# Attention and expert layers on one core: another order of the work between the last scores and the first expert tile

## The reference

```python
x = x + xattn(layernorm(x), ctx)      # 16 x 224 tokens of 512, context 16 x 750 of 384, 16 heads of 32
x = x + ffn(layernorm(x))
# ffn: logits = cos(x, centroids) + x @ w_route.T          (8 experts)
#      gates  = softmax over the top 2 of the logits
#      h      = gelu(x @ w1[e] + b1[e])                    (512 -> 256)
#      out    = sum over the two e of gates[e] * (h @ w2[e] + b2[e])
```

## Time and profile before

| | |
|---|---|
| median of 3 runs | 1463.79 us (1462.31 to 1467.72) |
| profiled execution, its own time | 1467.88 us |
| its span | 1466.0 us |
| mean granted clock of PE | 0.976 |
| PE busy | 1389.4 us (95% of the span) |
| PEld busy | 1109.4 us (76%) |
| POOL busy | 1082.7 us (74%) |
| DVE busy | 970.8 us (66%) |
| ACT busy | 840.8 us (57%) |
| from 1150 to 1200 us: PE, DVE, ACT, POOL busy | 35.5, 28.8, 29.6, 21.5 us of 50, granted clock 0.77 |

### The profile page before, as it was taken

The page is one execution under the profiler, slowest core; times in us unless marked ns, Lnnn a source line. Parts: engine busy times, 40 slices in busy tenths (PEclk is TensorE's granted clock), DMA queues, the critical chain, the costliest instruction groups (busy, mean ns, idle before and its releaser), DMA issues.

```text
span 1466.0 us, 34315 instructions
## 1 busy us (share of the span) xinstructions
PE 1389.4 (95%) x11524; PEld 1109.4 (76%) x11524; DVE 970.8 (66%) x1429; ACT 840.8 (57%) x1825; POOL 1082.7 (74%) x915
## 2 busy tenths in 40 slices
PE   4899999999999999999999999999999767999997
PEld 4777777787777787777777777777786446999986
DVE  6666767677676767677767676767667476444443
ACT  5546565666656566666665656665664552555554
POOL 3468787878787879797978787887877804776775
PEclk9989999999999999999999999999999687999999
DMA  7354545555454555555555554555454763887785
GB/s 242 90 130 109 166 128 154 149 136 156 124 155 123 161 137 140 140 140 139 142 145 154 134 156 124 167 132 152 118 136 125 243 128 75 146 144 131 144 143 85
DMA packets 134952, 206.74 MB, mean 141 GB/s; under 512 B 33808, under 2 KB 70832, under 8 KB 134656
## 3 DMA queue, kind: packets, MB, share of 16 engines
q1 hardware_dynamic: 120544, 173.20, 43.5%
q0 software_dynamic: 14240, 31.35, 11.9%
HBM read 64.29 MB, written 38.66 MB: 70 GB/s over the span
## 4 chain that ended last, share of the span: by engine, by line
PE 87%; DVE 5%; POOL 2%; issue 2%; DMA 2%; SPq 1%; ACT 1%; POOLq 0%; DVEq 0%; ACTq 0%
PE M L388 13%; PE S L1849 12%; PE M L389 12%; PE M L390 12%; PE O L1865 10%; PE M L1826 5%; PE M L2122 2%; PE M L2121 2%; PE M L2120 2%; PE M L2139 2%; PE M L2140 2%; PE M L2141 2%; PE S L2110 2%; PE M L1883 2%; POOL psum_p L634 1%
## 5 line engine op out<-in xcount | busy, mean ns | idle before, releaser
L634 POOL TENSOR_TENSOR psum_p<-psum_p,pr 125x896 f32<-125x896 f32 x254 | 549.8, 2165 | 107.5 <-ACT pr L917 82.1
L917 ACT ACTIVATE pr<-S 125x448 f32<-125x448 f32 x768 | 386.9, 542 | 205.2 <-PE S L1849 196.5
L1257 DVE TENSOR_REDUCE mx_parts<-M 112x2 f32<-112x1024 f32 x256 | 305.6, 1216 | 84.9 <-PE M L1826 84.8
L1849 PE MATMUL S<-qst,kst 128*125 128x224 f32 x1536 | 268.3, 289 | 5.4 <-ACT pr L917 3.2
L1849 PEld LDWEIGHTS S<-qst,kst 128*125 128x125 f32 x1536 | 223.6, 190 | 53.8 <-issue 22.1
L1865 PE MATMUL O<-pr,v 125*32 125x224 f32 x3072 | 185.4, 364 | 0.1
L1261 DVE TENSOR_REDUCE mx_parts<-M 112x4 f32<-112x952 f32 x128 | 141.0, 1143 | 59.6 <-PE M L1826 59.5
L631 POOL TENSOR_TENSOR psum_p<-pr 125x896 f32<-125x896 f32 x64 | 135.5, 2117 | 32.4 <-ACT pr L917 32.3
L388 PE MATMUL M<-ctx_h,wk_h 128*128 128x376 f32 (+1 forms) x384 | 136.2, 355 | 0.6 <-DVE mx_parts L1257 0.5
L389 PE MATMUL M<-ctx_l,wk_h 128*128 128x376 f32 (+1 forms) x384 | 129.9, 338 | 0.0
L885 ACT ACTIVATE kh_s<-M,bk_s 128x376 fp32r<-128x376 f32 (+1 forms) x128 | 73.1, 571 | 98.5 <-PE M L390 95.8
(11 more groups left out here) (259 smaller groups left out, 2999.9 us busy)
## 6 DMA issues: line engine op xcount, KB each, us to landing
kst<-kh_s SPq DMA_DIRECT2D x512, 93.8 KB, 2.2
kst<-kl_s SPq DMA_DIRECT2D x256, 93.8 KB, 2.2
ctx_r<-ctxT SPq DMA_DIRECT2D x48, 375.0 KB, 3.7
qst<-qh_s SPq DMA_DIRECT2D x128, 112.0 KB, 3.0
rows_d<-x_res SPq DMA_DIRECT2D x32, 448.0 KB, 4.7
w_l<-w SPq DMA_DIRECT2D x16, 512.0 KB, 7.7
x_ln<-x SPq DMA_DIRECT2D x17, 448.0 KB, 4.6
q_own<-qh_s SPq DMA_DIRECT2D x256, 28.0 KB, 1.8
```

The lines of the kernel that those rows point to most:

```text
L634: pool.tensor_tensor(out=total, in0=total, in1=tiles[half], op=ALU.add).then_inc(sum_step, 1)
L917: act.activation(pr[0:KP, (3 * g + p) % 2, j, :, :], S[0:KP, n % SB, 0:2 * NQ].rearrange("p (i n) -> p i n", i=2), ACT.Exp).then_inc(exp_d ...
L1257: dve.tensor_reduce(mx_parts[0:QP, pair, u, 0:1], M[0:QP, pair, 0:FIRST_KEYS], AX.X, ALU.max).then_inc(max_done, 1)
L1849: last = pe.matmul(S[0:KP, n % SB, NQ * h:NQ * (h + 1)], kst[:, i, j, o:o + KP], qst[:, i, j, :], start=True, stop=True)
```

## The change

Five edits, all between group 62 and the first expert tile:

- the last batch's two projections go into banks 0 and 2 in place of bank 4 one after the other;
- ACT makes the high parts of pieces 0 to 7 between the exponentials of groups 62 and 63 (`first_weights`, in `fourth(63)`), and of 8 to 15 in `after(64)`, where it made 0 to 10; DVE makes the remainders of 0 to 5 in `fourth(63)`, of 6 and 7 in `after(63)`, 8 in `after(64)`, 9 in `second(65)`; they stood in `after(64)` (0 to 3), `second(65)` (4) and behind the table (5 to 9);
- for the last batch `negate_identity` and `keep_parts` stand in front of `y_apply`, in `fourth(67)`;
- PE makes all six of its remainders behind the sums over tokens; two stood in front of them. ACT's exponential of the gap stands in front of their copies;
- `need` is computed behind the first tile's hidden remainder, not in front of the table's last steps; `landed` lies elsewhere for that.

Cut diff; each line is stripped of eight leading blanks.

```diff
@@ -86,7 +86,6 @@
...
 DVE_LOW = W_PIECES - PE_LOW
-ACT_EARLY = E + 3
 XG, YO = 6, 4
@@ -110,8 +109,8 @@
...
     order += [("X0", g + 1, None), ("K0", g + 2, 4), ("X1", g + 1, None), ("xT0", b + 1, 4),
-              ("K1", g + 2, 1), ("den", g - 1, 0), ("O0", b - 1, 4), ("X2", g + 1, None),
-              ("O1", b - 1, 4), ("xT1", b + 1, 0), ("mT", g + 1, 2), ("X0", g + 2, None)]
+              ("K1", g + 2, 1), ("den", g - 1, 0), ("O0", b - 1, 4 if b < B else 0), ("X2", g + 1, None),
+              ("O1", b - 1, 4 if b < B else 2), ("xT1", b + 1, 0), ("mT", g + 1, 2), ("X0", g + 2, None)]
 elif t == 2:
@@ -236,6 +235,7 @@
...
 above = in_a("above", [P, LC])
+landed = in_a("landed", [1, LC])
 empty, slot_f, later = in_a("empty", [P, LC]), in_a("slot_f", [P, LC]), in_a("later", [P, LC])
@@ -271,7 +271,7 @@
...
 in_p, end_p = region(first_of_at)
-past, landed = in_p("past", [1, LC, E - 1]), in_p("landed", [1, LC])
+past = in_p("past", [1, LC, E - 1])
 assert end_p[0] <= most_at
@@ -1006,6 +1006,14 @@
...

+        def first_weights(g, n):
+            if g == GROUPS - 1:
+                w_part(n)
+
+        def negate_identity():
+            wait_full(act, "O1", B - 1)
+            act.activation(minus_one[:, :], id_s[:, :], ACT.Copy, scale=-1.0).then_inc(masks, 1)
+
         def after(g):
@@ -1017,7 +1025,7 @@
...
                 act.wait_ge(b1_both, 32)
-                for n in range(ACT_EARLY):
+                for n in range(E, W_PIECES):
                     w_part(n)
@@ -1038,7 +1046,8 @@
...
             q_hi(g + 3)
-            keep_parts(b - 2)
+            if b - 2 < B - 1:
+                keep_parts(b - 2)
             max_out(g + 1)
@@ -1089,31 +1098,41 @@
...
             v_out(b + 1, 1)
+            first_weights(g, 0)
             exps(g - 1, 10)
...
             k_hi(g + 2, 0)
+            first_weights(g, 1)
             exps(g, 1)
...
             k_hi(g + 2, 1)
+            first_weights(g, 2)
             o_copy(g - 1)
             yT_part(b - 1, 0)
+            first_weights(g, 3)
             exps(g, 4)
             yT_part(b - 1, 1)
+            first_weights(g, 4)
             if b == B:
+                negate_identity()
+                keep_parts(b - 1)
                 y_apply(b - 1)
...
             v_out(b + 1, 2)
+            first_weights(g, 5)
             exps(g, 7)
...
             o_hi(g - 1)
+            first_weights(g, 6)
             exps(g, 9)
...
             v_out(b + 1, 3)
+            first_weights(g, 7)
             exps(g, 10)
@@ -1136,18 +1155,9 @@
...

-        wait_full(act, "O1", B - 1)
-        act.activation(minus_one[:, :], id_s[:, :], ACT.Copy, scale=-1.0).then_inc(masks, 1)
-        for n in range(ACT_EARLY, ACT_EARLY + 2):
-            w_part(n)
-        rest_part(0)
-        w_part(ACT_EARLY + 2)
         act.wait_ge(route, GAP_STEP)
         act.activation(gap[0:QP, :], gap[0:QP, :], ACT.Exp).then_inc(gap_exp, 1)
-        rest_part(1)
-        for n in range(ACT_EARLY + 3, W_PIECES):
-            w_part(n)
-        for k in range(2, PE_LOW):
+        for k in range(PE_LOW):
             rest_part(k)
@@ -1399,14 +1409,19 @@
...

+        def first_weights(g, n):
+            if g == GROUPS - 1:
+                w_part(n)
+
         def after(g):
...
                                   op=ALU.subtract).then_inc(freed("b1", 0), 1)
+                w_part(6)
+                w_part(7)
             if g == GROUPS:
-                for n in range(4):
-                    w_part(n)
+                w_part(E)
             if g == GROUPS + 2:
@@ -1446,7 +1461,7 @@
...
                 y_stats_half(B - 1, 0)
-                w_part(4)
+                w_part(E + 1)
             maximum(g + 1, 4)
@@ -1629,14 +1650,6 @@
...
         dve.tensor_reduce(landed[:, :], past[:, :, :], AX.X, ALU.add).then_inc(place, 1)
-        dve.wait_ge(place, 19)
-        for n in range(YO):
-            dve.tensor_scalar(need[:, n, :], landed[:, :], float(YO - 1 - n), None, ALU.add).then_inc(place, 1)
-        dve.wait_ge(place, 19 + YO)
-        dve.tensor_scalar(need[:, :, :], need[:, :, :], 2, None, ALU.logical_shift_right).then_inc(place, 1)
-        dve.wait_ge(place, 20 + YO)
-        dve.tensor_scalar(need[:, :, :], need[:, :, :], 16.0, 16.0, ALU.mult, ALU.add).then_inc(need_done, 1)
-
         dve.wait_ge(hot_used, 2 * CHUNKS)
@@ -1658,8 +1671,6 @@
...
         dve.tensor_copy(settled[:, :], ones[:, 0:1]).then_inc(table_done, 1)
-        for n in range(5, DVE_LOW):
-            w_part(n)

@@ -1687,6 +1698,13 @@
...
         h_low(0)
+        dve.wait_ge(place, 19)
+        for n in range(YO):
+            dve.tensor_scalar(need[:, n, :], landed[:, :], float(YO - 1 - n), None, ALU.add).then_inc(place, 1)
+        dve.wait_ge(place, 19 + YO)
+        dve.tensor_scalar(need[:, :, :], need[:, :, :], 2, None, ALU.logical_shift_right).then_inc(place, 1)
+        dve.wait_ge(place, 20 + YO)
+        dve.tensor_scalar(need[:, :, :], need[:, :, :], 16.0, 16.0, ALU.mult, ALU.add).then_inc(need_done, 1)
         dve.wait_ge(b2_in, 16)
@@ -2084,13 +2102,11 @@
...
         pe.wait_ge(masks, 2)
-        for k in range(2):
-            rest_part(k)
         pe.wait_ge(route, 12)
...
         pe.matmul(XT[0:QP, 0, 0:2 * TT * E], behind[0:QP, 0:QP], flat, start=True, stop=True).then_inc(sums_full, 1)
-        for k in range(2, PE_LOW):
+        for k in range(PE_LOW):
             rest_part(k)
...
```

## The result

The changed kernel takes **1468.38 us** (median of 20 runs, 1465.43 to 1472.05), the kernel before 1464.63 us (20 runs, 1461.84 to 1467.72). The profiled execution took 1467.89 us, its span 1466.1. The profiled execution of before had been a long one for its kernel (1467.88), so the two spans are nearly equal although the medians differ; its profile reached the point P, where the change begins to act, 2.2 us later. A checkpoint is given as P plus so many us.

The account below looks back on a forecast made before the run. PE alone bounds the expert loop, so only its start, set by a chain across engines, moves the end. Last logits +3.2, table +2.15, gathers -1.0 give +4.35 on 1463.8: 1468.1 us, range 1460 to 1473.5.

Parts of the forecast that it names:

- Step 1: Last groups' exponentials on ACT: eight weight parts and a 4.4 us wait for the first piece delay the last exponential, +8.7.
- Step 2: Last reciprocal on DVE: remainders and POOL's additions exclude each other and add their times, so it starts +11.3 us later.
- The alternative in the same step: Last reciprocal on DVE: without exclusion between DVE and POOL it follows the exponentials by 3.0 us, +7.5.
- The rule quoted in the prediction: DVE instructions with two SBUF inputs and POOL ones reading SBUF lock a shared port pair for whole instructions: +11.3, otherwise +7.5.
- Step 3: Last projections on PE: own banks let all 24 run in 7.2 us; second residual +5.9, worth 5.4 us against Step 2.
- Rival C: Slower: granted clock stays low through all 24 projections (+3.1) and the first two remainders (+2.0): 1473.2 us, chance 0.16.
- Step 4: Logits' copy ahead of the layer-norm pair on ACT: DVE's 2.68 us wait for PE goes, last logits +3.2.
- Step 5: Between routing and table: all six PE remainders behind the sums make PE late for the table, +2.15 us.
- Step 6: Gathers after the table: without weight parts beside them the first tile starts about 1.0 us sooner, -1.0 (bounds 0.5 and 1.2).
- Rival A: Not slower: additions and remainders interleave, so exclusion costs nothing; reciprocal at 1171.3, total +0.9, 1464.7 us, chance 0.2.

Follow-up runs that it names:

- e3: Changed kernel with two of PE's six remainders again in front of the sums: 1464.77 us, ratio 1.0001 to the kernel before.
- e4: Kernel before with only the weight parts moved on ACT and DVE; old banks, copy and PE order: 1473.15 us, ratio 1.0053.
- e6: Changed kernel with each of ACT's eight early weight parts one place later in its queue: 1469.67 us, ratio 1.0013 to the kernel before.
- e8: Kernel before with only the last copy of the logits' parts moved ahead of the layer-norm pair on ACT: 1466.51 us, ratio 0.9983.
- e1: Changed kernel with the weight parts on ACT and DVE back at their old places: 1461.66 us, ratio 0.9980 to the kernel before.
- e9: Last run told: the combined kernel with eight ACT weight parts, not eleven, ahead of the y copies: 1459.32 us, ratio 0.9958 to the kernel before.
- e2: Kernel before with only the own banks for the last two projections: 1461.85 us, ratio 0.9978.
- e7: Changed kernel with DVE's remainders 0 to 7 behind the table, ACT as changed: 1475.83 us in one profiled execution (kernel before: median 1469.29).
- the combined kernel: Changed kernel with weight parts back, two PE remainders before the sums, four DVE parts before the residuals: ratios 0.9966 and 0.9962 on two chips.
- e5: First run of the combined kernel, on the chip with the longer loop: 1463.43 us, ratio 0.9966 to the kernel before.
- e10: Second run of the combined kernel, unchanged, on another chip: 1459.22 us, ratio 0.9962 to the kernel before.

## Why the prediction was right, step by step

The time was forecast at 1468.1 and is 1468.4. The sum of the steps was +4.35; the first product shows +3.19 and the medians +3.75. That the time fits to 0.3 us is partly luck: the sum was 0.6 us too high, and the base, a median of 3 runs (1463.79), was 0.8 below that of 20 (1464.63). The steps did not all hold as well as that.

**Step 1** held: standstill 4.50 (4.4 was computed), last exponential +8.76 (+8.7). That the shift agrees to 0.1 us is chance, since the profile of before is early by up to 2 us against six others of the same work. The run with the parts one place later cuts the wait by 3.2 us and the end comes 3.6 sooner, one part of 0.95 included. The pieces land every 1.3 to 2.2 us (1.5 to 1.9 were put), and of the first eight parts only the first waits for its piece.

**Step 2** had the right mechanism and the wrong size; it is the failed term of the sum. Its queue of DVE and POOL from the eighth exponential on (8.65 us in the prediction) took 7.0: from POOL's start at 1162.29 to the end of `b_tl` at 1169.31. The step counted the part at 1161.49 in full (1.2 us), but that had begun before POOL's additions, and 0.4 of other work overlapped. The shift was +9.85, not +11.3. The alternative in the same step, +7.5, was wrong as well: it allowed 3.0 us from the last exponential to the reciprocal. Before, this took 4.21 (16.69 - 12.48), and in the run without DVE's early remainders it took 4.09. So without DVE's early parts the shift would be +8.6, and they cost 1.2 us with all that they meet, not 3.8. The rule quoted in the prediction from the Trainium skill, page "SBUF — State Buffer", section "SBUF: two separate sides", agrees with the rows: 5.89 us for two parts beside additions against 2.33 alone, the low part of O 1.86 against 0.45, an addition of 2.93 against 2.10. It gives nearly the right sum of the two engines' times: from 1162.29 to the end of `b_tl` the parts, the additions and the low part come to some 7.4 us at their lengths alone, and took 7.0. How much of it reaches the chain depends on who is late, which it doesn't tell.

**Step 3** held. Reciprocal to first projection 3.25 us (3.43 was computed, 4.28 before), projections 7.4 without a gap (7.2), and the difference between the shifts of the reciprocal and of the second residual is 9.85 - 4.48 = 5.4, as it was put. The +1.4 by which the residual was forecast too late is step 2's, carried on. Rival C, PE at the lower level throughout these matmuls, did not happen: 8 of 24 ran so. But how many do differs from profile to profile (by the lengths of the rows, 0.39 to 0.49 against 0.53 to 0.75): 15 before, 8 in after, e3, e4 and e6, 7 in e8, none in e1 and e9, 13 in e2 and e7, and in the combined kernel none on one chip and 13 on the other, 5.76 us against 8.35. That is 2.6 us between two executions of one kernel, and it is why single profiles of this stretch don't add up; some of the 5.4 us may be this too.

**Step 4** held: 5.16 us from the second residual to the last logits, DVE's own chain (5.23 was computed), 7.91 before. The last logits are 1.5 sooner than forecast, again by what step 2 was too high.

**Step 5** held closely: remainders end at 1210.62, T+16.0 (T+15.9), table T+23.6 (T+23.5). With two parts in front of the sums it is T+20.03, DVE alone (T+20.1; the small operations on `need` are six and not seven, the 1.05 us for them are right). The order on PE costs 3.6 us, and that gain went as it was said: DVE had less to do and PE came late in its place.

**Step 6** was too good: -1.0 was forecast, and from table to first product it is 8.99 us in place of 9.48, -0.5, the lower bound. POOL's gathers of after answer to the earlier trace rows:

```profile
1220.82 1.08 POOL L801 DMA_INDIRECT xg<-rows_d,table_x  x1 [41.10 <-DVE settled L1673]
1222.20 0.97 POOL L801 DMA_INDIRECT xg<-rows_d,table_x  x1 [0.30 <-issue]
```

The second gather is 0.97 as forecast (1.86 before), but what the first product waits for is mostly the first tile's rows, which hardly gain by it.

Rival A's time, 1464.7, was missed by 3.7 us. Its condition is that the exclusion costs nothing. The run without DVE's early remainders has the last logits at the same place as after (P+42.47 and P+42.34), but only because its projections ran slower, which may be chance; at the reciprocal it is 1.2 us sooner. So A was nearer to the size of the meeting than the forecast was, 0 and 3.8 against 1.2, and wrong in another number: it put 3.0 us between the last exponential and the reciprocal, where 4.1 were measured. Taken as 7.5 without the meeting and 3.8 with it, the forecast's +11.3 holds two errors of opposite sign, 1.1 too low and 2.6 too high; together they are the 1.45 by which step 2 came out too late.

## What to carry to other kernels

Work moved into an earlier stage is not free because an engine has idle time on average: on an in-order queue it waits for its own input with the critical work behind it, so put it where its data has landed already. Give idle time ahead of a dependency to work whose inputs are complete and which the late engine must do anyway (two parts before the sums: 3.6 us here), and make sure that no other move brings these inputs later, as in the last run. When several edits go in together, measure them apart: banks and copy gained here, and the weight parts and PE's order took back more than they gave. And compare a stretch over several profiles: the same kernel gave 5.76 and 8.35 us for one stretch of matmuls here.

## What the runs showed of the hardware

The meeting of DVE and POOL shows in both engines' rows as longer instructions, not as idle time: 5.89 us for two parts of 1.17 each, 2.93 for an addition of 2.10. A profile that reads busy time alone takes it for work.

The one-hot matmuls (64 columns, f16) take 3.82 to 3.86 us for 32 at both levels of the granted clock: in the windows view of before the clock is 1.00 in the first block's stretch and 0.54 in the second's, and both blocks take 3.82 (the earlier trace rows for the first, PE's timeline of before below for the second).

```profile
1206.00:1210.00 4.00, 3.44 (x31) 3.47 (x32) 3.97 (x6) 0.28 (x1) 0.00 (x0) 1.00 0.02 4
1210.00:1214.00 4.00, 3.01 (x28) 2.79 (x27) 3.96 (x7) 0.00 (x0) 0.00 (x0) 0.54 0.00 0
```

```profile
1211.37 3.82 PE L2100 MATMUL M<-hot_tok,hot_row 112*128 112x64 f16 x32 [0.99 <-DVE hot_row L1607]
```

(Columns of the first two lines: busy time of PE, PEld, DVE, ACT, POOL, then granted clock, share and rate of the DMA.) On the one chip where the loop took 5 us longer, PE has more idle time in it for which the profile shows no releaser: 2.4 us in e5 and 2.9 in e8, against 0.2 in e10. The granted clock from 1240 to 1440 us is 1.00 in all three. That is about half of the 5 us; the rest, and the reason, stay open.
